# 1/z moved from the scaled rows of h into the rounded attention weights; h split once a batch; x staged in a borrowed slot; first batch reordered (two GNN layers, 8 graphs, Trainium2, one core)

## The reference, cut to what matters

```python
h  = x @ W;  f1 = h @ a1;  f2 = h @ a2
e  = leaky_relu(f1 + f2^T, 0.2)
attention = softmax(adj * e, axis=1)
x1 = attention @ h + bias + x                     # layer 0
y  = adj @ (x1 @ W1 + b)                          # layer 1
y  = (y - mean) * rsqrt(var + 1e-5) * gamma + beta # mean, var over all 8 graphs
out = relu(y) + x1
```

## Time and profile before

| | us |
|---|---|
| median of 3 runs (lowest, highest) | 943.45 (942.08, 945.23) |
| the profiled execution: its own time | 945.52 |
| its span, first to last instruction | 943.7 |
| mean granted TensorE clock | 0.967 of full |

### The profile page before, as it was taken

The page is one execution under the profiler, slowest core; times in us unless marked ns, Lnnn a source line. Parts: engine busy times, 40 slices in busy tenths (PEclk is TensorE's granted clock), DMA queues, the critical chain, the costliest instruction groups (busy, mean ns, idle before and its releaser), DMA issues.

```text
span 943.7 us, 9327 instructions
## 1 busy us (share of the span) xinstructions
PE 885.1 (94%) x3167; PEld 557.4 (59%) x3167; DVE 715.6 (76%) x789; ACT 800.3 (85%) x619; POOL 293.2 (31%) x390
## 2 busy tenths in 40 slices
PE   7898999999999999999999999999999999999970
PEld 5333656675566756666566756667566666666850
DVE  1654677798678877798778977788777886789966
ACT  4897779997899979998899969999799987997745
POOL 0112241254223442272422641252521633235000
PEclk8999999999999999999999999999999999999995
DMA  8986474867567584766658574765757666565968
GB/s 320 422 342 224 167 274 169 309 224 268 196 241 266 178 321 170 272 248 223 265 217 296 201 307 158 261 242 196 306 189 274 248 224 230 184 232 184 421 285 334
DMA packets 48527, 238.03 MB, mean 252 GB/s; under 512 B 5816, under 2 KB 6440, under 8 KB 23904
## 3 DMA queue, kind: packets, MB, share of 16 engines
q1 hardware_dynamic: 48480, 237.44, 67.4%
HBM read 213.18 MB, written 24.23 MB: 252 GB/s over the span
## 4 chain that ended last, share of the span: by engine, by line
PE 79%; POOL 5%; DMA 4%; DVE 4%; issue 4%; ACT 1%; SPq 1%; DVEq 0%; ACTq 0%; POOLq 0%
PE acc L512 34%; PE acc L481 11%; PE acc L483 11%; PE acc L487 10%; PE acc L469 4%; DMA adj_slot<-adjT 3%; PE acc L493 3%; PE acc L446 3%; DVE scores L728 2%; POOL hz_lo L881 2%; POOL hz L866 2%; POOL hz_hi L878 2%; PE acc L525 1%; PE acc L528 1%; PE acc L527 1%
## 5 line engine op out<-in xcount | busy, mean ns | idle before, releaser
L749 DVE TENSOR_TENSOR exp_lo<-scores,hi 128x2048 fp32r<-128x2048 f32 (+1 forms) x133 | 273.9, 2072 | 123.7 <-ACT hi L622 123.4
L728 DVE CUSTOM_DVE_ANT_0 scores<-scores,adj_slot 128x2048 f32<-128x2048 f32 x128 | 298.8, 2334 | 50.2 <-ACT scores L601 21.6
L608 ACT ACTIVATE scores<-scores,neg_mx 128x2048 f32<-128x2048 f32 x128 | 255.8, 1998 | 26.9 <-DVE neg_mx L731 26.9
L622 ACT CAST hi<-scores 128x2048 fp32r<-128x2048 f32 (+1 forms) x133 | 214.9, 1631 | 63.1 <-PE acc L487 59.0
L601 ACT ACTIVATE scores<-adj_slot,f_cols 128x2048 f32<-128x2048 f32 x128 | 255.8, 2004 | 9.8 <-issue 5.2
L512 PE MATMUL acc<-adj_slot,region_even 128*128 128x512 f32 x512 | 228.7, 592 | 0.0
L512 PE MATMUL acc<-adj_slot,region_odd 128*128 128x512 f32 x392 | 175.3, 592 | 0.8 <-DVE region_odd L782 0.8
L481 PE MATMUL acc<-hi,hz_lo 128*128 128x512 f32 x448 | 161.1, 482 | 13.6 <-POOL hz_lo L881 13.6
L512 PEld LDWEIGHTS acc<-adj_slot,region_even 128*128 128x128 f32 x512 | 96.8, 190 | 100.0 <-issue 95.8
L481 PEld LDWEIGHTS acc<-hi,hz_lo 128*128 128x128 f32 x448 | 85.0, 191 | 73.8 <-issue 43.5
L483 PE MATMUL acc<-hi,hz_hi 128*128 128x512 f32 x448 | 124.8, 402 | 0.0
(11 more groups left out here) (76 smaller groups left out, 600.9 us busy)
## 6 DMA issues: line engine op xcount, KB each, us to landing
adj_slot<-adjT SPq DMA_DIRECT2D x151, 1024.0 KB, 4.9
adj_slot<-xT SPq DMA_DIRECT2D x12, 1024.0 KB, 9.8
adj_slot<-biasT SPq DMA_DIRECT2D x32, 256.0 KB, 6.4
xp_dram<-adj_slot SPq DMA_DIRECT2D x32, 256.0 KB, 2.5
adj_slot<-xp_dram SPq DMA_DIRECT2D x8, 1024.0 KB, 9.0
adj_slot<-f_rows SPq DMA_DIRECT2D x7, 1024.0 KB, 7.1
adj_slot<-y_dram SPq DMA_DIRECT2D x7, 1024.0 KB, 9.2
outT<-adj_slot SPq DMA_DIRECT2D x6, 1024.0 KB, 5.5
```

Source lines behind the costliest of these rows:

```text
L608: act.activation(scores[e][:, :], scores[e][:, :], ACT.Exp, bias=neg_mx[:, e:e + 1], accum_out=zsum[:, e:e + 1]).then_inc(exp_done, 1)
L622: act.copy(hi[m][:, part_cols(t, i)], scores[e][:, part_cols(t, i)]).then_inc(hi_done, 1)
L728: dve.tensor_tensor_reduce(scores[e][:, :], scores[e][:, :], slots[s][:, :], 1.0, NEG_BIG, ALU.mult, ALU.max, mx[:, e:e + 1]).then_inc(max ...
L749: dve.tensor_tensor(exp_lo[e][:, part_cols(t, i)], scores[e][:, part_cols(t, i)], hi[m][:, part_cols(t, i)].bitcast(F32), ALU.subtract).th ...
```

## The change

1. **1/z.** `exp_high` multiplies by `rz` while it rounds, and `exp_low` computes `scores * rz - hi` in one scalar_tensor_tensor. Both now need `rz` of their tile. POOL no longer scales h in batches 1 to 7: `split_h` makes a rounded copy and a low half of unscaled h, 256 columns at a time, eight times a batch, from `h_out` alone. Batch 0 still scales h.
2. **x.** The whole of x is loaded into slot 11 (`T_RES`) once `score(11)` has read it, `add_bias` works there after all of `split_h`, and the adj tile is loaded a second time for layer 1 (as tiles 8, 9 and 10 are already).
3. **Orders.** ACT: `edge(t+2)` before `exp_high(t)`, and the copies of h before `exp_high(0)` of the next batch. DVE: `exp_low(t-1)` in step t, except at both ends of a batch.
4. **Batch 0.** adj tiles come ahead of the x tiles in SP's queue, w1, b1, gamma and beta behind them; f2 of two tiles (not one) is made early; `rows_of_f` moves from tiles 0, 0, 1, 3, 5, 7, 8 to 1, 2, 3, 4, 6, 7, 9; DVE instead of ACT copies h and the rows of f out of PSUM; `add_bias` follows all 16 `scale_h`.

```diff
-    F_STEP = {1: 0, 2: 0, 3: 1, 4: 3, 5: 5, 6: 7, 7: 8}
+    X_AFTER = {1: 1, 2: 3, 3: 4, 4: 5, 5: 7, 6: 8, 7: 9}
+    F_STEP = {1: 1, 2: 2, 3: 3, 4: 4, 5: 6, 6: 7, 7: 9}
...
-            def load_residual(bt, c):
-
-                sp.wait_ge(hz_done, NT * bt.n + TC * (c + 1))
-                sp.dma_start(region[bt.par][:, cols(c)], xT[bt.n][:, cols(c)]).then_inc(x_loaded[c], 16)
+            def load_residual(bt):
+
+                sp.wait_ge(max_done, NT * bt.n + T_RES + 1)
+                sp.dma_start(res_sb[:, :], xT[bt.n]).then_inc(res_loaded, 16)
...
-                    pe.matmul(acc0[c][:, :], hz_hi[m][:, :], hi[m][:, cols(c)], start=False, stop=False)
...
+                    pe.matmul(acc0[c][:, :], half, hi[m][:, cols(c)], start=False, stop=False)
...
-                act.wait_ge(exp_done, NT * bt.n + t + 1)
+                act.wait_ge(rz_done, NT * bt.n + t + 1)
...
-                    act.copy(hi[m][:, part_cols(t, i)], scores[e][:, part_cols(t, i)]).then_inc(hi_done, 1)
+                    act.activation(hi[m][:, part_cols(t, i)], scores[e][:, part_cols(t, i)], ACT.Copy,
+                                   scale=rz[:, e:e + 1]).then_inc(hi_done, 1)
...
-                    dve.tensor_tensor(exp_lo[e][:, part_cols(t, i)], scores[e][:, part_cols(t, i)],
-                                      hi[m][:, part_cols(t, i)].bitcast(F32), ALU.subtract).then_inc(lo_done, 1)
+                    dve.scalar_tensor_tensor(exp_lo[e][:, part_cols(t, i)], scores[e][:, part_cols(t, i)],
+                                             rz[:, e:e + 1], hi[m][:, part_cols(t, i)].bitcast(F32),
+                                             ALU.mult, ALU.subtract).then_inc(lo_done, 1)
...
+            def split_h(bt, b):
+
+                r, block = h_ring(bt, b), slice(b * HB, (b + 1) * HB)
+                pool.wait_ge(h_out, NC * bt.n + b * HB // CH + 1)
+                if b >= ZR:
+                    wait_l0(pool, bt, TB * (b - ZR) + TB - 1)
+                elif bt.n > 1:
+                    wait_l0(pool, bt.prev(), TB * (b - ZR + NB) + TB - 1)
+                pool.tensor_copy(h_hi[r][:, :], region[bt.par][:, block]).then_inc(h_hi_done, 1)
+                pool.wait_ge(h_hi_done, NB * (bt.n - 1) + b + 1)
+                pool.tensor_tensor(h_lo[bt.par][:, block], region[bt.par][:, block], h_hi[r][:, :].bitcast(F32),
+                                   ALU.subtract).then_inc(h_lo_done, 1)
...
-                    if not is_first(bt):
+                    if not is_first(bt) and 1 < t < NT - 1:
+                        exp_low(bt, t - 1)
+                    if not is_first(bt) and (t == 0 or t >= NT - 2):
                         exp_low(bt, t)
```

More of the change, by code:

```diff
@@ L335, in step @@
                         load_adj(bt, t)
+                        for b in X_AFTER:
+                            if X_AFTER[b] == t and b == 1:
+                                sp.dma_start(x1_sb[:, :], xT[1]).then_inc(x1_loaded, 16)
+                            elif X_AFTER[b] == t:
+                                load_x(b, X_STAGE[b])
+                    sp.dma_start(w1_sb[:, :], W1).then_inc(w1_loaded, 16)
+                    sp.dma_start(b1_sb[:, :], b1.partition_broadcast(P)).then_inc(b1_loaded, 16)
+                    sp.dma_start(gb[:, 0:1], gamma).then_inc(gb_loaded, 16)
+                    sp.dma_start(gb[:, 1:2], beta).then_inc(gb_loaded, 16)
                     sp.wait_ge(row_out, 1)
@@ L344, in step @@
                     load_adj(nx, 1)
+                    load_f1(nx)
                     load_bias(bt)
-                    for c in range(NC - 1):
-                        load_residual(bt, c)
-                    load_f1(nx)
-                    load_residual(bt, NC - 1)
+                    load_residual(bt)
                 else:
@@ L486, in layer0_split @@
                     for c in part_chunks(t, i):
-                        l0_done(pe.matmul(acc0[c][:, :], hz_hi[m][:, :], exp_lo[e][:, cols(c)], start=False,
+                        l0_done(pe.matmul(acc0[c][:, :], half, exp_lo[e][:, cols(c)], start=False,
                                           stop=(t == NT - 1)), t, c)
@@ L491, in make_support @@
                 pe.wait_ge(xp_done, NC * bt.n + c + 1)
+                if is_first(bt) and c == 0:
+                    pe.wait_ge(w1_loaded, 16)
                 for q in range(TC):
@@ L641, in support_high, with h_from_psum @@
                     act.copy(sup_hi[:, cols(c)], region[bt.par][:, cols(c)]).then_inc(sup_hi_done, 1)
-            def h_from_psum(bt, banks, chunks=range(NC)):
-                for c in chunks:
+            def h_from_psum(bt, banks):
+                for c in range(NC):
                     act.wait_ge(h_mm, NC * bt.n + c + 1)
@@ L687, in _ @@
             edge(first, 1)
-            h_from_psum(first, acc0, [0, 1])
             steps(act, step)
@@ L792, in step @@
                         recip(bt, t)
+                    if is_first(bt) and t + 1 < NC:
+                        first_h(t + 1)
+                    if is_first(bt) and t == ROWS_STEP:
+                        rows_from_psum()
                     if is_first(bt) and t == TURN_STEP:
@@ L884, in add_bias @@
             def add_bias(bt, c):
-                pool.wait_ge(x_loaded[c], 16 * (bt.n + 1))
+                pool.wait_ge(res_loaded, 16 * (bt.n + 1))
                 pool.wait_ge(bias_loaded[c], 16 * (bt.n + 1))
-                pool.tensor_tensor(region[bt.par][:, cols(c)], region[bt.par][:, cols(c)], bias_sb[:, cols(c)], ALU.add)\
+                pool.tensor_tensor(res_sb[:, cols(c)], res_sb[:, cols(c)], bias_sb[:, cols(c)], ALU.add)\
                     .then_inc(xb_done, 1)
             def step(bt):
-                for t in range(NT):
-                    scale_h(bt, t)
-                    if t == 12:
-                        add_bias(bt, 0)
-                    if t == 14:
-                        add_bias(bt, 1)
@@ L897, in step @@
-                add_bias(bt, 2)
-                add_bias(bt, 3)
+                if is_first(bt):
+                    for t in range(NT):
+                        scale_h(bt, t)
+                else:
+                    for b in range(NB):
+                        split_h(bt, b)
+                for c in range(NC):
+                    add_bias(bt, c)
             pool.memset(ident[:, :], 0.0).then_inc(ident_set, 1)
```

135 lines of the change are left out of this document (65 added, 70 removed).

## The result

| | before | after |
|---|---|---|
| median, us (lowest, highest) | 944.34 (942.08, 946.03), 4 runs | 911.84 (910.58, 912.48), 4 runs |
| profiled execution, its own time | 945.52 | 911.96 |
| its span | 943.7 | 910.2 |
| mean granted TensorE clock | 0.967 | 0.984 |

The ratio after to before is 0.9656, with a 95% interval of 0.9631 to 0.968: faster by 32.5 us. The forecast was 910.9. In all sets two executions lie far outside the rest, one of the kernel before (1037.32 us) and one of the kernel of experiment 9 (2903.53 us, its matmuls three to four times as long), and count in no ratio.

What follows compares the result with a forecast made beforehand. PE's matmul time was taken as the bound, with losses where PE waits or runs at half clock. From 943.45: -24.5 (boundaries) + 3.5 (staged x) - 11.6 (batch 0) = -32.6, giving 910.9; range 904 to 918, reaching to 926 for rival one.

Steps and rivals of the forecast that it cites:

- The seven boundaries, 24.5 less 3.5: Start of batches 1 to 7: wait for `hz_lo` and half clock vanish, 24.5 us gained; staged x costs 3.5.
- The cost at the end of batches: Four `add_bias` together hold DVE at each batch's end: 0 to 1.3 us reach PE, taken as 0.5.
- Slack of `exp_low(1)`, 0.8: Start of batch 2: `exp_low(1)` on DVE ends at 232.3, PE wants it at 233.1.
- ACT's dearer form: `exp_high` on ACT with one pointer operand: 2.0 us, between 1900 and 2096 ns, hidden below PE's 6.17 a tile.
- scalar_tensor_tensor at 2.3: `exp_low` on DVE in its new form takes 2.3 us on 128x2048, no change.
- Rival two: scalar_tensor_tensor runs at half rate, 2.13 us more a tile, DVE becomes the bound: 1037 us; chance 13%.
- `split_h` at 0.7 free: POOL's copy and subtraction of 256 columns take 0.7 us free, 2.4 locked behind DVE; hidden behind PE's work.
- Batch 0, 11.6: Batch 0 up to the next h matmuls shortens from 98.04 to 86.4 us, 11.6 gained.
- tile 0 can follow at once: Batch 0: h matmuls end about 23.1, scaled h is ready, tile 0 runs without idle at 3.49, not 5.23.
- x may land at 87 unseen: End of batch 0: x landing as late as 87 us costs nothing, since `add_bias` ends before the last support.
- Rival one: Another wait of about 2 us a batch replaces the old one, or batch 0 gains nothing: 923 or 922; together 17%.
- Rival three: The boundary wait is only renamed, PE waiting for the rounded copy that now follows 1/z: 932 us; chance 2%.

Runs made afterwards that it cites:

- experiment 9: Changed kernel with second block of rows of f before tile 0, x asked for two tiles earlier, next batch's second adj tile loaded after x: 907.17 us, again 907.28.
- experiment 6: Changed kernel with one, then two, extra DVE multiplications by 1.0 ahead of each full `exp_low`: 956.15 us and 1079.66 us.
- experiment 7: Changed kernel with x asked for after layer 1 step 11 instead of 13: 911.69 us, ratio 0.9645 to the kernel before.

## Why the prediction was right, step by step

- **The seven boundaries, 24.5 less 3.5.** Right. By stage it had 18.0 for six batches and 3.0 for the rest; measured 18.5 and 3.9 (the 0.9 more in the rest isn't explained by any run). A batch takes 106.28 us against the 106.36 of the forecast, and PE's own 105.86 was met to 0.1 in the run with the 1/z part alone (105.8).
- **The cost at the end of batches**, taken as 0.5 of a range of 0 to 1.3. The mean excess is that (106.28 - 105.8 = 0.5), but 0.85 us of the six batches' 2.9 is the first boundary's wait for x, so the ends themselves cost 0.3 to 0.4 here; in the second trace of this kernel (experiment 9), without that wait, 106.26 - 105.8 gives 0.5. The cause is right in so far as PE waits for `exp_lo` there beside `add_bias`, and the batches fall to 105.95 in the trace where x comes earlier; the medians don't confirm it, and the waits themselves sum to only 0.7 us. How steeply this end gets dearer was not foreseen: see experiment 6.
- **Slack of `exp_low(1)`, 0.8.** Measured 218.75 against about 219.5: 0.75. It held.
- **ACT's dearer form**, taken as 2.0: 1996 ns. The Trainium skill's page "ScalarE: Activation LUTs", section "What ACT_TABLE_LOAD costs", gives some 93 ns for each pointer operand; the trace agrees, 1996 against 1900.
- **scalar_tensor_tensor at 2.3.** Right: 2.33 where POOL is quiet, 2484 ns on average. "No change" was a little short: the tensor_tensor that it replaced averaged 2360 ns in the kernel before, but the 124 ns were hidden. Rival two is out. The Trainium skill's page "Vector Engine (DVE) Microarchitecture Reference", section "Points that are easy to get wrong", has half throughput for this instruction with two SBUF sources that aren't bf16; with two fp32 SBUF sources and no accumulator output it ran at the speed of a tensor_tensor here, so the measurement decides against the rule for this form. The price of rival two was about right (1037; 1028 by the runs with extra work). Its threshold of 3.7 us held for the middle of a batch and not for the end, where 3.67 already cost 5.8 us a batch.
- **`split_h` at 0.7 free.** The copy took 0.40 and the subtraction 0.73; the means are 1.12 and 1.27 since most run beside DVE. Hidden, as said.
- **Batch 0, 11.6.** Measured 11.1, but by two errors that nearly cancel, so that this part of the hit is luck. The step that failed is "tile 0 can follow at once". I had the h matmuls ending at 23.1; they ended at 19.3, since they took 0.12 us each where the earlier trace rows has 0.21. The granted clock in the window 16.3 to 19.3 was 1.00, and 0.56 in 16.17 to 22.9 of the kernel before. So PE came early, found 1/z not ready (21.67, near the forecast's 21.9 for `hz`), idled 2.40 and paid the half clock that the forecast had struck out. Against the forecast, the start came 1.4 early and tile 0 took 1.75 more.
- **x may land at 87 unseen.** It landed at 87.92, and PE lost 0.85 us. The bound fits: in experiment 7, whose h matmuls come 0.4 later, x landed at 87.37 and the support took 3.74. But I had not priced a landing beyond it.
- **Rival one** holds in small: a wait for `exp_lo` does come at the end of batches, 0.16 us and not 2.
- **Rival three** is out: PE never waits for the rounded copy.
